# Causal attention in a four-stage transformer kernel: the mask leaves TensorE and is applied by VectorE in the maximum and by GpSimd after the exponential

## What is computed

```python
scores = jnp.einsum("bhqd,bhkd->bhqk", q, k_h) / math.sqrt(HEAD_DIM)
causal = jnp.triu(jnp.ones((t, t), dtype=bool), k=1)
scores = jnp.where(causal[None, None], jnp.finfo(scores.dtype).min, scores)
attn = jax.nn.softmax(scores, axis=-1)
ctx = jnp.einsum("bhqk,bhkd->bhqd", attn, v_h)
```

## Time and profile before

| | |
|---|---|
| median of three runs | 2404.42 us (2399.48 to 2405.88) |
| the profiled execution itself | 2407.62 us |
| its span, first to last instruction | 2405.8 us |
| TensorE matmul busy | 1945.4 us, 81% |
| VectorE busy | 1197.8 us, 50% |
| ScalarE busy | 917.6 us, 38% |
| GpSimd busy | 470.0 us, 20% |
| mean granted TensorE clock | 0.924 |

### The profile page before, as it was taken

How to read it: one execution, slowest core, us unless ns; L and a number is a source line. 1 busy time by engine, 2 the same in 40 slices (tenths; PEclk the granted TensorE clock), 3 DMA queues, 4 the chain that set the end, 5 groups by cost and what they waited for, 6 DMA issues and landing times. The chain is left out here.

```text
span 2405.8 us, 39049 instructions
## 1 busy us (share of the span) xinstructions
PE 1945.4 (81%) x13768; PEld 1378.8 (57%) x13768; DVE 1197.8 (50%) x2464; ACT 917.6 (38%) x1650; POOL 470.0 (20%) x1256
## 2 busy tenths in 40 slices
PE   4888978888873989987388888888788874889988
PEld 3555655555542766765365665565556552666766
DVE  4676566565544544543444544543554444544533
ACT  3444434444431433431344433443443441433522
POOL 3221121121100211212223211231221210201201
PEclk9899989989996999998699899998999996899999
DMA  2000100100106111010200000000001005110110
GB/s 89 1 1 1 54 2 1 54 1 3 34 1 216 36 53 33 19 35 36 84 1 1 28 14 15 27 1 28 1 19 32 5 1 190 62 53 13 39 35 18
DMA packets 35322, 80.54 MB, mean 33 GB/s; under 512 B 4362, under 2 KB 5002, under 8 KB 34644
## 3 DMA queue, kind: packets, MB, share of 16 engines
q1 hardware_dynamic: 35156, 78.29, 9.8%
HBM read 61.50 MB, written 16.78 MB: 33 GB/s over the span
## 5 line engine op out<-in xcount | busy, mean ns | idle before, releaser
L245 PE MATMUL f_ring<-f_xt,f_codes 128*128 128x512 f32 (+1 forms) x1408 | 360.3, 399 | 25.0 <-DVE f_codes L1263 25.0
L245 PEld LDWEIGHTS f_ring<-f_xt,f_codes 128*128 128x128 f32 (+1 forms) x1408 | 266.0, 189 | 91.6 <-issue 26.2
L711 ACT ACTIVATE ab_region<-ab_scores 128x512 f32<-128x512 f32 x320 | 190.1, 600 | 141.7 <-PE ab_scores L891 140.8
L711 ACT ACTIVATE aa_region<-aa_scores 128x512 f32<-128x512 f32 x320 | 184.8, 598 | 128.3 <-PE aa_scores L891 124.3
L1159 POOL TENSOR_TENSOR f_ht<-f_work,f_ht 128x512 fp32r<-128x512 f32 (+1 forms) x88 | 113.4, 1293 | 580.9 <-ACT f_ht L1211 580.9
L796 DVE TENSOR_REDUCE ab_nmax<-ab_maxima 128x1 f32<-128x384 f32 (+1 forms) x256 | 149.1, 618 | 140.5 <-PE ab_maxima L891 137.9
L1284 DVE TENSOR_TENSOR f_work<-f_ring,f_work 128x512 f32<-128x512 f32 (+1 forms) x176 | 121.6, 691 | 172.2 <-ACT f_work L1200 148.2
L245 PE MATMUL f_ring<-f_dcodes,f_ht 128*128 128x512 f32 (+1 forms) x704 | 183.5, 418 | 17.6 <-DVE f_raw L1324 16.6
L890 PE MATMUL aa_maxima<-aa_stacks 96*128 96x128 bf16 (+3 forms) x512 | 144.3, 326 | 42.7 <-DVE aa_nmax L796 29.6
L1200 ACT ACTIVATE f_work<-f_ring,f_scales 128x512 f32<-128x512 f32 (+1 forms) x176 | 120.5, 685 | 144.0 <-PE f_ring L245 144.0
L245 PEld LDWEIGHTS f_ring<-f_dcodes,f_ht 128*128 128x128 f32 (+1 forms) x704 | 138.8, 200 | 57.6 <-DVE f_raw L1324 20.1
(11 more groups left out here) (185 smaller groups left out, 3657.6 us busy)
## 6 DMA issues: line engine op xcount, KB each, us to landing
f_x<-mid SPq DMA_DIRECT2D x32, 256.0 KB, 3.1
f_raw<-mid SPq DMA_DIRECT2D x32, 256.0 KB, 4.2
f_raw<-in_gate_q SPq DMA_DIRECT2D x8, 688.0 KB, 6.5
f_raw<-in_up_q SPq DMA_DIRECT2D x8, 688.0 KB, 5.6
f_raw<-in_down_q SPq DMA_DIRECT2D x10, 512.0 KB, 4.8
aa_x<-in_x SPq DMA_DIRECT2D x16, 256.0 KB, 3.1
aa_res<-in_x SPq DMA_DIRECT2D x16, 256.0 KB, 3.0
mid<-aa_res SPq DMA_DIRECT2D x16, 256.0 KB, 2.1
```

The source lines that it names most:

```text
L245: mm = pe.matmul(out, w, x, start=start and i == 0, stop=stop and i == len(pairs) - 1)
L711: act.activation(probs[:, s // 2 % 2, SUB * (s % 2) + i, :], scores[:, sbk, :], ACT.Exp, scale=0.25).then_inc(scores_freed[sbk].sem, 1)
```

## The change

Both kinds of mask product are removed. The maximum is taken by one VectorE instruction that adds the mask (now as wide as a row of keys, zero but for its last 128 columns, in bf16 in SBUF), writes the masked scores back to their PSUM bank and delivers their maximum as a second output, no longer negated; the rows of ones become rows of -1 instead. The exponential is taken of the unmasked scores, and GpSimd then sets the entries above the diagonal to zero in SBUF, a 128x128 block at a time (`causal`, at the end of every step of its list). The value products wait for GpSimd (`cut_off`) where they waited for ScalarE. A semaphore increment stands ahead of each `reduce_max`, behind its waits.

```diff
-    mask_qk = ctx.enter_context(nc.sbuf_tensor("mask_qk", [P, P], BF16))
-    mask_kq = ctx.enter_context(nc.sbuf_tensor("mask_kq", [P, P], BF16))
+    mask = ctx.enter_context(nc.sbuf_tensor("mask", [P, T], BF16))
...
-            pool.memset(stacks[MAXROW:ROWS, :, HU:NST, :], 1.0).then_inc(ones_set, 1)
+            pool.memset(stacks[MAXROW:ROWS, :, HU:NST, :], -1.0).then_inc(ones_set, 1)
...
+            def causal(b, s, i):
+
+                sbk, nth = i % 3, SB[i % 3] * s + i // 3
+                chunk = probs[:, s // 2 % 2, SUB * (s % 2) + i, :]
+                blocks = ((0,), (0,), (0, 384), (0, 384), (0, 256))[i]
+                pool.wait_ge(scores_freed[sbk].sem, scores_freed[sbk].at(b, nth + 1))
+                pool.sem_inc(waited, 1)
+                for at in blocks:
+                    last = pool.affine_select(out=chunk[:, at:at + P], in_=chunk[:, at:at + P],
+                                              compare_op=ALU.is_ge, fill=0.0, base=0, pattern=[[1, P]],
+                                              channel_multiplier=-1)
+                last.then_inc(cut_off.sem, 1)
...
                         if 5 in ks and after is not None:
                             split_max(*after)
+                        causal(b0 + bs, s, i)
...
-                nm, h, src = nmax[:, s % 2], k % 2, maxima[:, mb, :]
-                if k < 2:
-                    dve.tensor_reduce(nm[:, 0, h:h + 1], src[:, 0:P], AX_X, ALU.max, negate=True)
-                    last = dve.tensor_reduce(nm[:, 1, h:h + 1], src[:, P:3 * P], AX_X, ALU.max, negate=True)
-                else:
-                    qt = 1 + k // 2
-                    last = dve.tensor_reduce(nm[:, qt, h:h + 1], src[:, 0:(qt + 1) * P], AX_X, ALU.max,
-                                             negate=True)
+                nm, h, src = rowmax[:, s % 2], k % 2, maxima[:, mb, :]
+                dve.sem_inc(dve_waited, 1)
+                for qt in ((0, 1) if k < 2 else (1 + k // 2,)):
+                    n, at = (qt + 1) * P, P if qt == 1 else 0
+                    last = dve.tensor_tensor_reduce(out=src[:, at:at + n], in0=src[:, at:at + n],
+                                                    in1=mask[:, T - n:T], scale=1.0, scalar=MASKED,
+                                                    op0=ALU.add, op1=ALU.max, accum_out=nm[:, qt, h:h + 1])
...
-                    mm = block_scores(maxima[:, mb, at:at + n], st[0:STK, h, qt * P:(qt + 1) * P],
-                                      st[0:STK, hk, 0:n], mask_qk, qt * P)
+                    mm = pe.matmul(maxima[:, mb, at:at + n], st[0:STK, h, qt * P:(qt + 1) * P],
+                                   st[0:STK, hk, 0:n], start=True, stop=True)
...
-                    mm = block_scores(scores[:, sbk, at:at + n], st[:, hk, kb * P:(kb + 1) * P],
-                                      st[:, h, kb * P:T], mask_kq, 0)
+                    mm = pe.matmul(scores[:, sbk, at:at + n], st[:, hk, kb * P:(kb + 1) * P], st[:, h, kb * P:T],
+                                   start=True, stop=True)
...
-                pe.wait_ge(scores_freed[1].sem, scores_freed[1].at(b, SB[1] * (2 * n + 2)))
+                pe.wait_ge(cut_off.sem, cut_off.at(b, 2 * SUB * (n + 1)))
```

More of the change, by code:

```diff
@@ L144, in _ @@
             pool.memset(identb[:], 0.0)
-            pool.memset(mask_qk[:], 0.0)
-            pool.memset(mask_kq[:], 0.0).then_inc(made, 1)
+            pool.memset(mask[:], 0.0).then_inc(made, 1)
             pool.wait_ge(made, 1)
@@ L150, in _ @@
                                    pattern=[[-1, P]], channel_multiplier=1)
[L152 to L158, removed]
+            pool.affine_select(out=mask[:, T - P:T], in_=mask[:, T - P:T], compare_op=ALU.is_ge, fill=MASKED,
+                               base=0, pattern=[[-1, P]], channel_multiplier=1)
+    return identf, identb, mask
 class Norm:
@@ L361, in attention @@
               rope_dram=None, bias_dram=None, biassel_dram=None):
-    identf, identb, mask_qk, mask_kq = consts
+    identf, identb, mask = consts
     rope, biased = rope_dram is not None, bias_dram is not None
@@ L406, in attention @@
         power = sb("power", [P, 1], F32)
-        nmax = sb("nmax", [P, 2, NT, 2], F32)
+        rowmax = sb("rowmax", [P, 2, NT, 2], F32)
         nrest = sb("nrest", [P, 2, NT, 2], F32)
@@ L447, in attention @@
         replicated = Signal(sem("replicated"), UT)
-        waited = sem("pool_waited")
+        waited, dve_waited = sem("pool_waited"), sem("dve_waited")
+        cut_off = Signal(sem("cut_off"), SUB * PAIRS)
         nmax_chain = Signal(sem("nmax_chain"), 3 * PAIRS)
@@ L578, in split_max @@
             def split_max(b, s):
-                nm, nr, np_ = nmax[:, s % 2], nrest[:, s % 2], nparts[:, s % 2]
+                nm, nr, np_ = rowmax[:, s % 2], nrest[:, s % 2], nparts[:, s % 2]
                 pool.wait_ge(maxima_freed[1].sem, maxima_freed[1].at(b, MB[1] * (s + 1)))
@@ L886, in project @@
                 return passes(pe, out, pairs)
[L888 to L892, removed]
             def max_scores(b, s, k):
```

## The result

The changed kernel takes 2555.69 us (2537.6 to 2559.78, four runs) against 2405.15 us: ratio 1.061 [1.055, 1.067]. The forecast was 2434 us in a range of 2365 to 2530. The direction was right, the size a fifth of the measured one, and the time lies above the range. The profiled execution took 2558.06 us, with a span of 2556.3 us.

A forecast was written before the change was run, and what follows sets the result against it. VectorE's reductions were taken to bound the first part of each attention pair, TensorE the rest. Product savings against second-output and increment costs gave +29.2 us, with the ends +30.4, on a 2404.4 us median: forecast 2434, range 2365 to 2530.

The forecast's parts named there:

- The reading of the waits: Both attentions: the bound changes within a pair, VectorE's reductions first, TensorE for the rest; TensorE waited for the split 26 and 33 times.
- the short pairs: Attention pairs where TensorE waits for GpSimd's split: a 6.36 us loop holding all eight reductions and no mask product.
- The read-out: VectorE's masked reduction: writing out the accumulator was expected to be a second instruction, for which the page gives no duration.
- The selections: GpSimd zeroing the triangle, eight a pair at 0.25 us: counted at nothing except 1.2 us at the attentions' ends.
- the sum: Both attentions, by kind of pair: products' gain against costs on VectorE, together +29.2 us, with the ends +30.4.
- e: VectorE's reductions: cost of the masked instruction's second output, 0.07 us each, weighted with 791 reductions on the path.
- w: The semaphore increment ahead of a reduction: 0.12 us once a pair where VectorE waits, otherwise 0.
- Rivals 4 and 5: On VectorE's masked reduction: 4, second output waits for drain, 2498 to 2553 us, chance 0.12; 5, half rate, about 2697, 0.06.
- rival 6: Attentions: GpSimd becomes the bound, 2465 us, or the granted clock falls, at most 24 us; chance 0.04 for either.
- the late splits: GpSimd in the attentions: the split stands behind late selections; two of them in 59 pairs give +30 us.
- The masked pass: VectorE's masked reduction: priced like the plain one, 285, 413, 552 and 683 ns for 128 to 512 columns.
- rival 1: VectorE's second output is free or nearly so, under 0.023 us: faster, 2364 to 2397 us; chance 0.27.

The follow-up runs named there:

- read-out (stand-in): Kernel before with a one-column copy behind each of the 1024 reductions, the copy freeing the bank, no increment added; 2469.65 us, ratio 1.026.
- before with added products: Kernel before with 272 throwaway score products put where TensorE waits for the split maxima; 2404.88 us, ratio 0.999.

## Why the prediction was wrong

**What held.** The reading of the waits: the short pairs are a loop of reductions, split, transposes and row copy without a product (with no products at all its shortest took 6.43 us, at a clock of 0.96, where before had 6.36). VectorE's cost in it: 6.36 was to become about 6.9 us, and at a clock of 1.00 it was 6.83. The read-out is two instructions. The selections cost next to nothing. The direction held, in part by luck: the sum had its plus from e and w alone, and it counted as a gain the products whose removal cost 47 us by itself. Rivals 4 and 5 fell: the next pass begins with the read instead of after it, and 512 columns take 712 ns and not near 1200. Of rival 6 the late splits fell, while the fall of the clock came true, far larger than its price. The measured time lies beside rival 4's upper end (2553 us) by chance.

**The step that failed** is "a product removed gives 0.06 us where TensorE decides and nothing in the other part". With e and w at nothing it gave -40 us; the run with no products and no new cost measured +47. In the part where TensorE waits, the products cost no time but were work, and without them the granted clock fell to the low level. The dense work behind the wait paid for that, and so did the loop itself, whose transposes and score products are TensorE's: 7.21 us without products, at 0.50, where before had 6.36. I had the clock in rival 6, as "two hundredths" and "at most 24 us", with a bound taken from nothing in the trace; it fell by twelve hundredths in the attentions. The Trainium skill has the mechanism (TensorE: Matmul & The Clock Gate, What's actually happening): the default state is the throttled one, and activity releases it. The runs agree: the short pair at 1.00 with its products and at 0.82 without.

**Terms mis-sized.** w was put at 0.12 us once a pair, 15 us. The price of one was right (0.11), the count wrong: the short waits for TensorE within a pair each show it, and alone it measured 36 us. The masked pass was priced like the plain one; written back to PSUM it is 12 to 52 ns longer in aa, worth about 9 us there.

**Right by luck.** e = 0.07 was taken from a small instruction that holds the engine for 0.07 us. The read-out doesn't do that. The 68 to 111 ns by which a bank comes free later are the write to PSUM for the most part; with the scores in SBUF 9 to 15 ns are left, which is below rival 1's 0.023 us, and aa was still slower than before.

**The account.** Each cost alone, against before: products gone +47, increment +36, read-out (stand-in) +61, selections +7 (within the noise); together 151, measured 150. That they add so well is luck and no proof: each of these numbers holds some lost clock, the pass's own lengthening is in none, the copy isn't the read, and in the short pair they don't add. There the increment alone makes 6.72 us of 6.36 and the copies alone 6.73, but the changed kernel with both of its costs has 6.83 at the same clock. Inside the changed kernel the missing products cost less than alone: putting them back takes the ratio from 1.061 to 1.046, some 36 us, not 47.

**What stays open.** Over the whole kernel, lost clock and longer chains weren't separated, neither in the 36 and 61 us (clocks of 0.912 and 0.909) nor in the 150; the short loop, with 0.88 of 1.35 us, is the one place where they are. The changed kernel without the increment wasn't tried. And the two feed-forward phases, the same in all kernels, took 922 to 928 us together in the profiles of before, before with added products, increment alone and second column alone, but 929 to 941 us in the ten others, with a lower clock; why wasn't looked into, and it is 17 of the 150 us.

## What to carry to other kernels

Work on TensorE that sits in a wait isn't free to remove: look at the granted clock in the stretch behind it, and price the removal at the low level as a case of its own. Before a cheap product is traded for a second output on the engine that frees the PSUM banks, count how many of those instructions lie between TensorE's waits, and see where the second output and the main one are written. A semaphore increment ahead of a small instruction cost 0.11 us here each time the instruction had to wait for its input, and nothing where the input was there; short waits don't show as idling in merged rows, so compare the distances between starts. And compare a loop at one level of the clock: what looks like the price of an instruction can be mostly the clock.

## What was unexpected of the hardware

- Taking 2048 products off TensorE and adding nothing made the program 1.9% slower, its clock going from 0.924 to 0.859.
- A VectorE pass that writes the PSUM bank that it reads takes 712 ns for 512 columns and 465 for 256; written to SBUF it takes 686 and 420, and the read behind it 83 ns in place of 134.
- A loop of 6.36 us in which TensorE mostly waits took 7.21 us when it did less work, at a clock of 0.50; with new work for VectorE it took 6.83 us at 1.00 and 7.71 at 0.61.
- A read of the accumulator lasts 134 ns, but the next pass can begin with it (1478.65 and 1478.66).
